# Ternary feed-forward of a two-layer decoder: order of transposes and down product, ScalarE takes off the rounding constant, GpSimd normalises the tokens

## The reference

```python
def _act_quant(x):
    scale = 127.0 / jnp.clip(jnp.max(jnp.abs(x), axis=-1, keepdims=True), 1e-05)
    return jnp.clip(jnp.round(x * scale), -128.0, 127.0) / scale
def _bitlinear(x, w):
    return jnp.einsum('bsi,oi->bso', _act_quant(x), _weight_quant(w))
gate = jax.nn.silu(_bitlinear(x, w_gate))        # x: layer-normalised tokens, 256 -> 1024
up = _bitlinear(x, w_up)
x = x + _bitlinear(gate * up, w_down)            # 1024 -> 256
```

## Time and profile of the kernel before

| | |
|---|---|
| median of three runs | 5153.24 us |
| the profiled execution | 5163.71 us |
| its span, first to last instruction | 5161.9 us |
| TensorE matmul busy over the span | 4819.2 us, 93% |
| VectorE busy | 3661.8 us, 71% |
| ScalarE busy | 2882.3 us, 56% |
| GpSimd busy | 2638.7 us, 51% |
| mean granted TensorE clock | 0.967 of full speed |

### The profile page before, as it was taken

One profiled execution on the slowest core, in us unless ns is written; L12 is line 12 of the kernel. 1 busy time (PEld: TensorE's weight loads), 2 busy tenths in 40 slices (PEclk: granted clock), 3 DMA queues, 4 the chain that ended last, 5 costly groups with the idle time before them and its releaser, 6 DMA issues. The chain is left out here.

```text
span 5161.9 us, 71163 instructions
## 1 busy us (share of the span) xinstructions
PE 4819.2 (93%) x24010; PEld 2644.1 (51%) x24010; DVE 3661.8 (71%) x6559; ACT 2882.3 (56%) x6256; POOL 2638.7 (51%) x1567
## 2 busy tenths in 40 slices
PE   6899997899999897899879999999999999999976
PEld 5555555344444596344545555555555555555533
DVE  8677776788888587788646766666676666666668
ACT  5666663477777643577535444454444445454457
POOL 5556554100000251530147878777787877778740
PEclk9899998899999998799989999999999999999989
DMA  6567668422222005332544333333434333343300
GB/s 216 195 238 245 241 241 234 130 80 78 67 73 75 1 1 209 102 97 79 165 129 98 84 92 90 86 95 81 100 80 95 89 87 91 85 101 75 90 17 29
DMA packets 344186, 576.28 MB, mean 112 GB/s; under 512 B 49120, under 2 KB 142368, under 8 KB 342800
## 3 DMA queue, kind: packets, MB, share of 16 engines
q1 hardware_dynamic: 341616, 567.53, 38.6%
q10 hardware_dynamic: 2208, 4.20, 0.2%
HBM read 335.54 MB, written 201.85 MB: 104 GB/s over the span
## 5 line engine op out<-in xcount | busy, mean ns | idle before, releaser
L3005 POOL TENSOR_TENSOR la_acc<-la_acc,la_pr 128x1024 f32<-128x1024 f32 x704 | 1697.3, 2411 | 444.8 <-ACT la_pr L2964 404.6
L2964 ACT ACTIVATE la_pr<-la_s_ps 128x512 f32<-128x512 f32 x1536 | 793.9, 603 | 961.2 <-PE la_s_ps L2813 960.3
L2820 PE MATMUL la_o_ps<-la_pr,lw_vf 128*64 128x512 f32 x3072 | 743.8, 605 | 0.0
L2812 PE MATMUL la_s_ps<-la_q_hl,lw_k_hh 128*128 128x512 f32 x1536 | 692.1, 451 | 1.8 <-ACT la_q_hs L2940 1.4
L1909 DVE TENSOR_REDUCE ca_mx<-ca_m_ps 128x2 f32<-128x1024 f32 x512 | 600.7, 1217 | 116.1 <-PE ca_m_ps L1769 116.1
L3026 DVE TENSOR_REDUCE la_mx<-la_m_ps 128x2 f32<-128x1024 f32 x384 | 462.9, 1205 | 296.3 <-PE la_m_ps L2795 288.2
L1871 ACT ACTIVATE ca_pr<-ca_s_ps 128x512 f32<-128x512 f32 x1024 | 541.9, 601 | 203.0 <-PE ca_s_ps L1776 199.6
L2813 PE MATMUL la_s_ps<-la_q_hs,lw_k_l 65*128 65x512 f32 x1536 | 609.0, 396 | 0.0
L3026 DVE TENSOR_REDUCE la_mx<-la_misc 128x2 f32<-128x1024 f32 x384 | 466.2, 1214 | 1.3 <-PE la_misc L2795 1.3
L2812 PEld LDWEIGHTS la_s_ps<-la_q_hl,lw_k_hh 128*128 128x128 f32 x1536 | 290.1, 189 | 279.5 <-issue 137.0
L2820 PEld LDWEIGHTS la_o_ps<-la_pr,lw_vf 128*64 128x64 f32 x3072 | 186.2, 136 | 346.5 <-issue 245.3
(11 more groups left out here) (414 smaller groups left out, 8760.7 us busy)
## 6 DMA issues: line engine op xcount, KB each, us to landing
lw_k_hh<-scratch_k_high SPq DMA_DIRECT2D x128, 512.0 KB, 6.5
scratch_k_high<-sc_k_high SPq DMA_DIRECT2D x128, 256.0 KB, 2.7
scratch_k_low<-sc_k_low SPq DMA_DIRECT2D x128, 256.0 KB, 2.8
lw_w_parts<-scratch_w_parts SPq DMA_DIRECT2D x64, 512.0 KB, 6.1
lw_k_l<-scratch_k_low SPq DMA_DIRECT2D x64, 512.0 KB, 8.5
lw_vf<-scratch_xv SPq DMA_DIRECT2D x64, 512.0 KB, 4.3
cl_ks<-scratch_k_rows SPq DMA_DIRECT2D x384, 64.0 KB, 2.7
scratch_vaug<-sc_v SPq DMA_DIRECT2D x16, 1024.0 KB, 4.4
```

What stands on the lines that cost most here:

```text
L2812: pe.matmul(s_ps[:, bank, :], k_hh[:, par, h, keys], q_hl[:, par, h, :], start=True, stop=False)
L2820: last = pe.matmul(o_ps[XD * h:XD * h + XD, :], vf[:, par, st, XD * h:XD * h + XD], pr[:, st % LAG, h, :], start=(st == 0), stop=(st == XT ...
L2964: act.activation(pr[:, st % LAG, h, :], s_ps[:, (2 * st + h) % 3, :], ACT.Exp, scale=scale).then_inc(p_done, 1)
L3005: pool.tensor_tensor(total, total, exps, ALU.add).then_inc(acc_done, 1)
```

## The change

It touches only `ternary_ffn`, in three parts.

The hidden row: `hidden_integers` and `hq` are gone. `turn_hidden` transposes the float32 `hr` (now two buffers) with the float32 identity into a float32 `ht_ps`, and `keep_hidden` takes ROUND off while it copies to bf16, with an activation whose bias is a new constant `unround`.

The order in iteration n: TensorE runs `turn_hidden(n-1)`, `gate(n+1)`, `up(n+1)`, `down(n-1)`, in slot 2 `turn_tokens`. ScalarE runs `keep_hidden(n-1)`, in slot 3 `keep_tokens`, `gate(n+1)`, `round_hidden(n)`, in slot 2 `round_tokens`. VectorE keeps its order without `hidden_integers`. LAG stays at 2 for `finish`.

The tokens: ScalarE's `apply` is gone. GpSimd multiplies by `rstd` and then adds `shift`, with eight operations of 128x256 a batch, behind its small operations of that batch.

```diff
--- before.py
+++ after.py
@@ -3106,13 +3106,13 @@
         unit = pool_.sb("unit", [P, 2, 2, NT])
         gated = pool_.sb("gated", [P, 2, INNER])
         h = pool_.sb("h", [P, 2, INNER])
-        hr = pool_.sb("hr", [P, INNER])
-        hq = pool_.sb("hq", [P, 2, INNER], BF16)
+        hr = pool_.sb("hr", [P, 2, INNER])
         hqT = pool_.sb("hqT", [P, KI, P], BF16)
         hmax = pool_.sb("hmax", [P, 1])
         hinv = pool_.sb("hinv", [P, 2])
         hunit = pool_.sb("hunit", [P, 2])
         round_c = pool_.sb("round_c", [P, 1])
+        unround = pool_.sb("unround", [P, 1])
         scaled = pool_.sb("scaled", [P, NT])
         shift = pool_.sb("shift", [P, NT])
         zeros = pool_.sb("zeros", [P, NT])
@@ -3120,17 +3120,17 @@
         tp = pool_.ps("tp", [P, KD, T], BF16)
         g_ps = pool_.ps("g_ps", [P, 2, T])
         u_ps = pool_.ps("u_ps", [P, 2, T])
-        ht_ps = pool_.ps("ht_ps", [P, KI, P], BF16)
+        ht_ps = pool_.ps("ht_ps", [P, KI, P])
         y_ps = pool_.ps("y_ps", [P, T])
         w_loaded = sems(nc, semctx, "tf", "gate_loaded up_loaded down_loaded")
         (xstep, xround, xq_done, tp_ready, xT_done, g_ready, u_ready, gated_done, h_done,
-         hstep, hr_done, hq_done, ht_ready, hT_done, y_ready, x_done, out_stored, constants_set, scaled_done, shift_done, xn_done) = sems(
+         hstep, hr_done, ht_ready, hT_done, y_ready, x_done, out_stored, constants_set, scaled_done, shift_done, xn_scaled, xn_done) = sems(
             nc, semctx, "tf", "xstep xround xq_done tp_ready xT_done g_ready u_ready gated_done h_done "
-            "hstep hr_done hq_done ht_ready hT_done y_ready x_done out_stored constants_set scaled_done shift_done xn_done")
+            "hstep hr_done ht_ready hT_done y_ready x_done out_stored constants_set scaled_done shift_done xn_scaled xn_done")
         HSTEPS = 4
         XSTEPS = 5
         TILES, LAG = NT * B, 2
-        MOMENTS, APPLY, UNITS, INTEGERS, TOKENS = 3, 0, 1, 2, 3
+        MOMENTS, UNITS, INTEGERS, TOKENS = 3, 1, 2, 3
 
         def of(n, slot, ahead=1):
 
@@ -3179,10 +3179,10 @@
                     return last
 
                 def turn_hidden(n):
-                    pe.wait_ge(hq_done, n + 1)
+                    pe.wait_ge(hr_done, n + 1)
                     pe.wait_ge(hT_done, n)
                     for k in range(KI):
-                        last = pe.transpose(ht_ps[:, k, :], hq[:, n % 2, k * P:(k + 1) * P], g.ident_bf[:, :])
+                        last = pe.transpose(ht_ps[:, k, :], hr[:, n % 2, k * P:(k + 1) * P], g.ident[:, :])
                     last.then_inc(ht_ready, 1)
 
                 def down(n):
@@ -3198,29 +3198,20 @@
                 pe.wait_ge(w_loaded[1], 16)
                 up(0)
                 for n in range(TILES + LAG):
-                    if n >= LAG:
-                        if n == LAG:
-                            pe.wait_ge(w_loaded[2], 16)
-                        down(n - LAG)
+                    if 0 < n <= TILES:
+                        turn_hidden(n - 1)
                     if n + 1 < TILES:
                         gate(n + 1)
                         up(n + 1)
                     if 0 < n <= TILES:
-                        turn_hidden(n - 1)
+                        if n == 1:
+                            pe.wait_ge(w_loaded[2], 16)
+                        down(n - 1)
                     if of(n, INTEGERS) is not None:
                         turn_tokens(of(n, INTEGERS))
 
             @block.scalar
             def _(act):
-                def apply(b):
-
-                    act.wait_ge(shift_done, b + 1)
-                    act.wait_ge(xstep, max(XSTEPS * (b - 1) + 1, 0))
-                    act.wait_ge(xround, NT * b)
-                    for j in range(NT):
-                        act.activation(xn[:, j, :], g.x[:, b * NT + j, :], ACT.Identity, bias=shift[:, j:j + 1],
-                                       scale=norm.rstd[:, j:j + 1]).then_inc(xn_done, 1)
-
                 def round_tokens(b):
                     act.wait_ge(xstep, XSTEPS * b + 3)
                     act.wait_ge(xq_done, b)
@@ -3244,33 +3235,31 @@
 
                 def round_hidden(n):
                     act.wait_ge(hstep, HSTEPS * n + 3)
-                    act.wait_ge(hq_done, n)
-                    act.activation(hr[:, :], h[:, n % 2, :], ACT.Identity, bias=round_c[:, 0:1],
+                    if n > 1:
+                        act.wait_ge(ht_ready, n - 1)
+                    act.activation(hr[:, n % 2, :], h[:, n % 2, :], ACT.Identity, bias=round_c[:, 0:1],
                                    scale=hinv[:, n % 2:n % 2 + 1]).then_inc(hr_done, 1)
 
                 def keep_hidden(n):
                     act.wait_ge(ht_ready, n + 1)
                     act.wait_ge(y_ready, n)
-                    act.activation(hqT[:, :, :], ht_ps[:, :, :], ACT.Copy).then_inc(hT_done, 1)
-
-                act.wait_ge(constants_set, 2)
-                apply(0)
+                    act.activation(hqT[:, :, :], ht_ps[:, :, :], ACT.Identity, bias=unround[:, 0:1]).then_inc(hT_done, 1)
+
+                act.wait_ge(constants_set, 3)
                 round_tokens(0)
                 keep_tokens(0)
                 gate(0)
                 for n in range(TILES + LAG):
                     if 0 < n <= TILES:
-                        round_hidden(n - 1)
-                    if of(n, INTEGERS) is not None:
-                        round_tokens(of(n, INTEGERS))
+                        keep_hidden(n - 1)
                     if of(n, TOKENS) is not None:
                         keep_tokens(of(n, TOKENS))
                     if n + 1 < TILES:
                         gate(n + 1)
-                    if of(n, APPLY) is not None:
-                        apply(of(n, APPLY))
-                    if 0 < n <= TILES:
-                        keep_hidden(n - 1)
+                    if n < TILES:
+                        round_hidden(n)
+                    if of(n, INTEGERS) is not None:
+                        round_tokens(of(n, INTEGERS))
 
             @block.gpsimd
             def _(pool):
@@ -3284,6 +3273,14 @@
                     pool.wait_ge(scaled_done, b + 1)
                     pool.wait_ge(constants_set, 1)
                     pool.tensor_tensor(shift[:, :], zeros[:, :], scaled[:, :], ALU.subtract).then_inc(shift_done, 1)
+                    pool.wait_ge(shift_done, b + 1)
+                    pool.wait_ge(xstep, max(XSTEPS * (b - 1) + 1, 0))
+                    pool.wait_ge(xround, NT * b)
+                    for j in range(NT):
+                        pool.tensor_scalar(xn[:, j, :], g.x[:, b * NT + j, :], norm.rstd[:, j:j + 1], None, ALU.mult).then_inc(xn_scaled, 1)
+                    for j in range(NT):
+                        pool.wait_ge(xn_scaled, NT * b + j + 1)
+                        pool.tensor_scalar(xn[:, j, :], xn[:, j, :], shift[:, j:j + 1], None, ALU.add).then_inc(xn_done, 1)
 
             @block.vector
             def _(dve):
@@ -3335,12 +3332,6 @@
                         dve.wait_ge(x_done, n - 1)
                     dve.tensor_scalar(hunit[:, n % 2:n % 2 + 1], hmax[:, :], wmean[:, 2:3], None, ALU.mult).then_inc(hstep, 1)
 
-                def hidden_integers(n):
-                    dve.wait_ge(hr_done, n + 1)
-                    if n > 1:
-                        dve.wait_ge(ht_ready, n - 1)
-                    dve.tensor_scalar(hq[:, n % 2, :], hr[:, :], ROUND, QMAX, ALU.subtract, ALU.min).then_inc(hq_done, 1)
-
                 def finish(n):
                     dve.wait_ge(y_ready, n + 1)
                     dve.wait_ge(hstep, HSTEPS * (n + 1))
@@ -3349,6 +3340,7 @@
                                              op0=ALU.mult, op1=ALU.add).then_inc(x_done, 1)
 
                 dve.memset(round_c[:, :], ROUND).then_inc(constants_set, 1)
+                dve.memset(unround[:, :], -ROUND).then_inc(constants_set, 1)
                 moments(0)
                 token_maxima(0)
                 token_units(0)
@@ -3359,8 +3351,6 @@
                         hidden(n)
                     if n >= LAG:
                         finish(n - LAG)
-                    if 0 < n <= TILES:
-                        hidden_integers(n - 1)
                     if n < TILES:
                         hidden_units(n)
                     if of(n, UNITS) is not None:
```

## The result

The changed kernel takes 5178.64 us (median of 6 runs, 5170.56 to 5184.2); the kernel before 5155.37 beside it. The ratio is 1.0041, with a 95% interval of 1.0031 to 1.0051: slower by about 21 us. The forecast was 5166.2, with a range from 5152 to 5180. The profiled execution spans 5173.9 us, 12 us more than that of before, and the rest of the 21 hides ahead of the phase: in this execution the phase began 9.6 us earlier than in that of before, after the same instructions. So the executions scatter outside the phase.

What follows compares the result with a forecast made beforehand. No engine was full, so a chain passing between engines was taken to set the pace. Terms -1.2 -0.9 +10.5 -1.3 +5 +0.9 = +13.0 us on a median of 5153.2 gave 5166.2, range 5152 to 5180.

Steps and rivals of the forecast that it cites:

- plain tiles: Tiles without token steps: from 4.33 to 4.29 us each, -1.2 us over 31 tiles.
- start: Start of the phase: GpSimd's operations 3.4 against 2.07, but apply(1) and hidden_integers(0) leave the path; -1.3 us.
- The walk of the loop: Plain tile in the new order: copy, gate, rounding on ScalarE set the pace, 4.29 us; copy 0 dearer.
- a sign of being wrong: The forecast is wrong if the float32 transposes take more than 1.04 us at the full clock.
- The slots: Token steps in slots 0 to 3: 5.4 us a batch in place of 3.9, +10.5 in seven batches.
- GpSimd's estimate of 0.36 us: GpSimd's normalisation: 0.36 us per 256-element operation, 3.4 for eight with gaps, hidden in the loop.
- the third rival: GpSimd at the dear price: start 4.4 us later, loop up to 0.5 to 1 a batch; sum +22, chance 0.07.
- The clock term: Low TensorE clock after the token gaps: 1.3 us a batch, 9 less the 4 of before, +5.
- The second rival: Every batch pays both low-clock parts, 2.7 us: sum +23, 5176; chance 0.12.
- The end: Last tile's transposes at the low clock would take 1.97 us instead of 1.03: +0.9.
- The first rival: The clock drops no more often than before: sum +4 to +8, about 5159; chance 0.27.
- the rival of TensorE's pace: TensorE's 3.40 us paces the loop rather than ScalarE's chain: sum -15, 5138; chance 0.06.

Runs made afterwards that it cites:

- e5: Changed kernel with idle TensorE products filling the gaps ahead of the token transposes and the slot 3 gate product; 1.0026 of the kernel before, phase 208.4 us.
- e8: Changed kernel with a plain copy in keep_hidden that leaves the rounding constant in; phase 215.0 us, one execution only.
- e11: Changed kernel with token steps spread, GpSimd's multiply and add fused, and the constant taken off by a copy with immediate bias; 0.9947 of the kernel before.
- e6: Changed kernel with round_tokens ahead of gate and round_hidden in ScalarE's slot 2 queue; 1.0030 of the kernel before, phase 205.1 us.
- e4: Changed kernel with turn_tokens behind the next turn_hidden on TensorE instead of ahead of it; 1.0030 of the kernel before, phase 208.5 us.
- e1: Kernel before with the float32 hidden row alone, old queue order and old normalisation; 1.0010 of the kernel before, phase 203.7 us.
- e2: Changed kernel with the tokens normalised by ScalarE again; 1.0057 of the kernel before, phase 219.2 us.
- e9: Changed kernel with GpSimd's multiply and add in one instruction, four a batch instead of eight; 1.0032 of the kernel before, phase 208.4 us.
- e3: Kernel before with GpSimd's eight normalising operations in place of apply, nothing else changed; 1.0019 of the kernel before, phase 203.1 us.
- e7: Changed kernel with token steps spread into ScalarE's idle time and the first batch normalised by ScalarE; 0.9975 of the kernel before, phase 179.9 us.

## Why the prediction was right, and where it was off

The direction and the mechanism were right, and the time, 5178.64, lay inside the range, 1.4 below its upper end: +21.6 in the phase against a forecast of +13.0. The two terms that were mis-sized most, the plain tile and the start, both erred by 4 us and the same way. Term by term:

| term | forecast | measured |
|---|---|---|
| plain tiles, 31 of them | -1.2 (4.29 each) | +3 (4.42 to 4.43 each) |
| last tile without a gate | -0.9 | -0.9 (3.43 for 4.33, from e5) |
| token steps at the full clock, seven batches | +10.5 (5.4 each for 3.9) | +9.4 (5.24, from one batch) |
| start | -1.3 | +2.8 |
| clock | +5 | +6.6 (10.6 less 4) |
| GpSimd in the loop | 0 | +0.4 (one batch) |
| end | +0.9 | +0.2 |

The rows of the token steps and of the clock rest on the one batch at the full clock and on the estimate of 173.0 made from it. The measured column adds up to 21.5.

- The walk of the loop was right: copy, gate, rounding, transposes. Mis-sized was the copy. I took none of the 0 to 0.09 more, "because both copies are plain functions". The new one isn't plain: it has a bias column, and e8 and e11 price that at 0.09 us. The float32 transposes of a plain tile were 1.09 rather than 1.04, which the prediction had named as a sign of being wrong. Together 0.13 a tile, 4 us.
- The slots were right in place and size. VectorE's integers waited 24.3 us in seven batches (3.5 each, near 3 forecast), TensorE 23.5 and 14.8 (3.4 and 2.1 each, 3.4 and 2.2 forecast). e6 undid one link and got about 8 back at the full clock; e4 undid another and ran into GpSimd; e1 against e2 put 15.5 on the order.
- GpSimd's estimate of 0.36 us for 256 elements failed: 0.93, the price of the third rival. The step was to choose the multiply with an add as the nearest row, for single operations. Its form with two operations was what made it quick (e9). The trace of the kernel before had a row of a single operation, a minimum with an immediate, which I passed over; it stands below this list. At 2.7 ns an element it is much nearer to the 3.6 that came than the 1.1 of the row I took. The rival's start was right to half a microsecond (+4.4, and 4.1 came). Its loop term (0.5 to 1 a batch) came only once in the changed kernel: in the batch of the timeline above the tokens were there at 5105.12 and the maxima began at 5106.85. The low clock had made room for them; where the batch was shorter, in e3, e4, e5 and e7, VectorE waited for GpSimd in six batches each. That the forecast's 0 for the loop nearly held is luck: it stood on a price of 0.36.
- The clock term was near (9 forecast for the changed kernel, 10.6 by the estimate). The second rival (2.7 in every batch) did not come: against full-clock tiles two batches paid 3.1 and 2.4, four between 0.9 and 1.6, and one, near 5070, nothing. The token transposes behind the first gap ran low in three batches (0.87, 1.03 and 1.03 us against 0.62), the gate product behind the second gap in three (1.89 against 1.04). In two batches, near 5020 and 5044, both started at the full clock, and it fell only later in the batch. The Trainium skill says that such bursts start at the low clock each time (TensorE: Matmul & The Clock Gate, "HAM oscillation — how this bites in real kernels"); the trace agrees for 6 of 14 gaps.
- The end was right in its cause and not in its sum. The last transposes ran low as forecast (1.90), but the down product behind them ran at the full clock, where that of before had taken 1.89; the two lines stand below as well.
- The first rival (clock as before) is refuted by the rows 0.94 and 0.89, the rival of TensorE's pace by the plain tile of 4.42.

The row of the single GpSimd operation in the kernel before:

```profile
L2100 POOL TENSOR_SCALAR tw_q<-tw_raw 128x1024 bf16<-128x1024 f32 x6 | 16.5, 2770 | 0.2
```

The last hidden transposes and the last down product of the changed kernel:

```profile
5166.32 1.90 PE L3185 MATMUL tf_ht_ps<-g_ident,tf_hr 128*128 128x128 f32 x8
...
5169.43 1.05 PE L3192 MATMUL tf_y_ps<-tf_wq,tf_hqT 128*128 128x256 bf16 x8 [1.21 <-ACT tf_hqT L3246]
```

What remains open: why the clock fell behind some of the gaps and not behind others of the same length; how the phases of e2, e4, e5, e6 and e9 would scatter over several executions; and e4 with GpSimd's fused operation, which would show what its edit is worth without the wait for GpSimd, was not run.

## What to carry to other kernels

When a step is moved in a queue, follow what stands behind it on every engine: here one call behind another on ScalarE held VectorE and TensorE for 3 us a batch, and the loop grew although VectorE had been rid of 0.68 us in each of 32 tiles. Look for each engine's idle stretch in the new loop and put the side work there, in pieces that fit: this turned a loss of 21 us into a gain of 13, and with two cheaper instruction forms into 27. Expect a slow step to hide behind another loss: here GpSimd's price showed at the start alone, until e4, e5 and e7 made the batch shorter, and then it took a part of each gain. Price an operation by a row of its very form (one or two operations, column or immediate operand), not by its function and size.

## What the runs showed of the hardware

- GpSimd's `tensor_scalar` with one operation (multiply or add by a column) on 128x256 float32 takes 927 ns in the changed kernel, with multiply and add and two column operands 555 ns (e9).
- ScalarE's copy of 128x1024 out of PSUM takes 1.02 us from bf16 (before) or float32 (e8), also with an immediate bias (e11), and 1.11 with a bias column (changed).
- GpSimd and VectorE slow each other: with VectorE's float32-to-bf16 `tensor_scalar` in the loop (e3) GpSimd's operations took 1001 ns instead of 927, and `hq` 723 instead of 684, on average 6 to 8% more; the longest took 1405 and 932. The Trainium skill (GPSIMD Engine Reference, section "1. Specifications") says that the two share their SBUF interfaces, and that GpSimd contends with VectorE's instructions that run in a mode with two ports or have two SBUF inputs. The trace agrees that the two slow each other; in which mode `hq` ran no run shows.
- A TensorE kept busy in two gaps of 3.4 and 2.1 us a batch held the full clock for the whole loop (e5); with those gaps empty it fell to 0.89 on average, though not behind every gap.
